# Turning v into token order: four TensorE transposes and a ScalarE copy, against a VectorE block transpose and a trip through DRAM

## The chip, the cores and the metric

The kernel runs on one NeuronCore of one Trainium2 chip. The time is the device time of one execution of the program in microseconds (us). Five instruction streams run side by side and meet through semaphores: TensorE (PE in the rows, its weight loads PEld), VectorE (DVE), ScalarE (ACT), GpSimd (POOL) and SyncE (SP, whose instructions here are almost all DMA issues, SPq in the rows).

## The reference, cut to what matters

```python
q = silu(x @ Wq); k = silu(x @ Wk); v = silu(x @ Wv); z = x @ Wz      # x: 2048 tokens x 512, W: 512 x 2048
q, k, v = causal_conv4(q), causal_conv4(k), causal_conv4(v)           # depthwise, 4 taps
q, k = rope(q), rope(k);  q, k = q / |q|, k / |k|                     # 16 heads of 128
out = 0
for s in range(4):                                                    # the token itself and 3 before it
    attn = einsum("bshd,bshd->bsh", q, lag(k, s)) * scale
    out = out + (attn * sigmoid(lag(a, s) * b))[..., None] * lag(v, s)
out = out * rms(out) * norm_w * silu(z)
s = out @ Wout
x = x + s * silu(ffn(xn))                                             # xn: layernorm of x; the x above is xn too
```

## The kernel before, in words

The work on q, k, v, z and the attention is done in 64 steps: for each of 16 heads `h` four groups `g` of 512 tokens, `c = 4h + g`. Heads 0, 1 and 15 are written out, heads 2 to 14 are one hardware loop with four steps in its body. In such a step the channels of a head lie on the 128 partitions and the 512 tokens along the free dimension. After the 64 steps follow the feed-forward part and the output projection, which the change leaves alone.

Every engine has a hand-written order of its own for a step (`step` in `on_sync`, `on_gpsimd`, `on_scalar`, `on_vector`, `on_tensor`), and the steps overlap: while q, k and v of step c are made, the rest of the steps c-1, c-2 and c-3 is done.

- TensorE, step c: twelve matmuls each for q, k and v (`project`, L982; operands split in a high and a low part), `turn_fold` (L1050, four transposes of summed squares, c-1), twelve for z (c-2), `turn_v` (L1026, four transposes of v, c-1), `sum_values` (L1038, c-3, in two halves of a matrix bank), `score` (L1060, c-2). Then q of step c+1.
- ScalarE: SiLU of the q bank into `u_q` (L636), the first tap into `y_q` (L651); the same for k and v; squares of q and k, SiLU of z, `copy_v` (L668: the transposed v from its bank into `v_tok`), a small spill.
- VectorE: the taps 1 to 3 of q, 1 to 3 of k, 1 and 2 of v (L800), and between them the three parts of rope (L820, L824, L827), `sum_fold` (L833), `gate_scores` and `mask_band` (L841 and L850, which make `coef`, the weights of `sum_values`), `join_out` and `make_o` (L806, L858), and at g = 1 and 3 the low parts of the next weights (L811: z at g = 1, q, k and v at g = 3).
- GpSimd: adds the fourth tap to `y_v` and sums squares, both by an accumulating DMA; makes norms and `gates` (L534).
- SyncE: the half swaps of q and k for rope (L425), the reciprocal norms through a DRAM scratch and back (`store_rq` L392 to L395, `load_rq` L402, whose result `gates` is made from), `o_buf` to DRAM (`store_o`, L406), next weights (L411).

`sum_values` of step c multiplies `v_tok` of c-3 with `coef` of c-3, and `coef` is made by VectorE in the same step c:

```python
wait(pe, coef_done, c - 2)
wait(pe, v_tok_done, c - 2)
wait(pe, o_done, c - 3)
wait(pe, out_sq_done, c - 3)
```

Inside the hardware loop `c` is a register, so the value that such a wait compares with has to be computed by an instruction of the engine's own sequencer (REGISTER_ALU or ISA in the rows of instructions); values already at hand in a register are used again.

Of the kernel before, what the change touches and what calls it, by code (L numbers as in the profile page):

```python
# [6 lines left out]
def gated_recurrent_block_kernel(  # L7
# [64 lines left out]
    o_scratch = nc.dram_tensor("o_scratch", [HD, S], fp32).ap()  # L72
    rq_scratch = nc.dram_tensor("rq_scratch", [G, P + LAGS, BC], fp32).ap()
# [131 lines left out]
def attention(nc, env):  # L205
# [10 lines left out]
     ones, ones_set, o_stored, o_done, out_sq_done, sq_added, rq_scratch, ffn) = (  # L216
# [4 lines left out]
                         "sq_added", "rq_scratch", "ffn"))  # L221
# [5 lines left out]
    HALF = D // 2  # L227
    bank_qv, bank_kz = banks[0], banks[1]
    bank_tqv, bank_tk = banks[2], banks[3]
# [74 lines left out]
    turned_v = sem("turned_v")  # L304
    norms_done = sem("norms_done")
    v_tok_done = sem("v_tok_done")
# [23 lines left out]
    last_tap_added = sem("last_tap_added")  # L330

# [29 lines left out]
    def on_sync(sp):  # L361
# [41 lines left out]

        def store_o(h3, g3, k):
# [8 lines left out]
        def step(h, g):  # L413
# [38 lines left out]
    def on_gpsimd(pool):  # L452
# [89 lines left out]
        def add_last_tap(g1, c):  # L542
            wait(pool, last_tap_made, c)
            wait(pool, conv_done["v"], 2 * c)
            wait(pool, turned_v, c - 1)
# [35 lines left out]
    def on_scalar(act):  # L581
# [51 lines left out]
        def silu_and_tap(n, bank, h, g, c):  # L633
# [6 lines left out]
            if n == "v":  # L640
                wait(act, last_tap_added, 16 * (c - 1))
                wait(act, turned_v, c - 1)
# [21 lines left out]

        def copy_v(g1, c):
            wait(act, turned_v, c)
            wait(act, out_done, c - 3)
            nc.scalar.activation(v_tok[:, g1 * BC:(g1 + 1) * BC, :],  # L668
                                 bank_tqv[:, :].rearrange("p (b d) -> p b d", b=BC),
                                 ACT.Copy).then_inc(v_tok_done, 1)  # L670
# [29 lines left out]
        def step(h, g):  # L700
# [15 lines left out]
            if at := back(h, g, 1):  # L716
                copy_v(at[1], c)
# [21 lines left out]
        copy_v(G - 1, NC)  # L739
# [19 lines left out]
    def on_vector(dve):  # L759
# [76 lines left out]

        def gate_scores(g2, k):
# [25 lines left out]
        def step(h, g):  # L863
# [39 lines left out]
            conv_tap("v", 1, h, g, c)  # L903
            if is_start(h, g):
# [27 lines left out]
        schedule(dve, step)  # L932
        rope("k", 1, G - 1, NC - 1)
# [20 lines left out]
    def on_tensor(pe):  # L954
# [64 lines left out]
        def turn_v(g1, c):  # L1019
            wait(pe, v_tok_done, c - 1)  # L1020
            if isinstance(c, int) and c == NC:
                pe.wait_ge(conv_done["v"], 2 * NC + 1)
# [581 lines left out]
```

## Time and profile before

| | |
|---|---|
| median of 3 runs | 1341.99 us (1341.51 to 1342.49) |
| profiled execution | 1341.58 us |
| span of its instructions | 1339.8 us |
| PE busy | 1316.8 us, 98% |
| DVE busy | 956.3 us, 71% |
| ACT busy | 782.0 us, 58% |
| POOL busy | 472.3 us, 35% |
| DMA engines, all queues | 31.9% SyncE's, 22.2% GpSimd's |

The span runs from the first instruction to the last, and the 1.8 us between it and the profiled time lie around it. Busy shares are means over stages that differ: the 64 steps end at about 925 us, and in them VectorE is busy 90% of the time, after them far less. PE's clock is granted in full throughout.

### The profile page before, as it was taken

To read this page: it belongs to the slowest core of one execution; us is meant where nothing else is said; L and a number is where in the kernel's file an instruction comes from. 1 tells how busy PE (TensorE), PEld (TensorE's weight loads), DVE (VectorE), ACT (ScalarE), POOL (GpSimd) and SP (SyncE) were. 2 spreads that over 40 slices of the span, in tenths; PEclk is the share of its full clock that TensorE was granted. 3 is DMA by queue.
4 is the path that set the end of the run, shared out by engine and by line. 5 is a ranking of instruction groups with operands and counts; after the bars stand their busy time and mean duration, and the time that the engine had idled before them with its cause. 6 is when DMAs were issued, how large, how long until landed. Compare 5 with 4: busy or idle time off the path is not lost.

```text
span 1339.8 us, 22528 instructions
## 1 busy us (share of the span) xinstructions
PE 1316.8 (98%) x6568; PEld 1102.9 (82%) x6568; DVE 956.3 (71%) x1531; ACT 782.0 (58%) x1504; POOL 472.3 (35%) x634
## 2 busy tenths in 40 slices
PE   7999999999999999999999999999999999999998
PEld 5688888888888888888888888887888888888886
DVE  7898999989998999889998999986122222324442
ACT  5676766667666766667676776665544434422221
POOL 6254545544544544545554455543000000000001
PEclk9999999999999999999999999999999999999999
DMA  8366667566666566565666657556610101256543
GB/s 264 85 126 132 135 123 154 129 128 138 134 138 146 120 136 148 121 147 121 146 139 130 139 118 158 105 121 172 207 40 24 47 16 55 70 166 206 179 131 137
DMA packets 141562, 171.83 MB, mean 128 GB/s; under 512 B 32720, under 2 KB 69584, under 8 KB 141264
## 3 DMA queue, kind: packets, MB, share of 16 engines
q1 hardware_dynamic: 114160, 121.48, 31.9%
q0 software_dynamic: 27360, 49.82, 22.2%
q8 instruction: 23, 0.38, 0.1%
q14 instruction: 19, 0.16, 0.0%
HBM read 62.58 MB, written 25.30 MB: 66 GB/s over the span
## 4 chain that ended last, share of the span: by engine, by line
PE 95%; DVE 1%; issue 1%; DMA 1%; POOL 1%; ACT 1%; SPq 0%; POOLq 0%; DVEq 0%; ACTq 0%
PE bank L982 50%; PE bank L1489 13%; PE bank L1292 9%; PE bank L1279 8%; PE bank L1038 4%; PE bank L1060 4%; PE bank L1050 2%; PE bank L1026 2%; PE bank L972 1%; DMA down_raw<-in_x 1%; PE bank L959 0%; PE bank L998 0%; POOL rnorm L510 0%; DMA down_raw<-down_raw 0%; PE bank L120 0%
## 5 line engine op out<-in xcount | busy, mean ns | idle before, releaser
L800 DVE SCALAR_TENSOR_TENSOR y_q<-u_q,cw_q,y_q 128x512 f32<-128x512 f32 x192 | 143.1, 745 | 70.9 <-ACT y_q L651 70.7
L1268 DVE TENSOR_TENSOR hid_lo<-relu,hid_hi 128x512 fp32r<-128x512 f32 x64 | 44.3, 693 | 168.2 <-ACT hid_hi L1260 168.1
L800 DVE SCALAR_TENSOR_TENSOR y_k<-u_k,cw_k,y_k 128x512 f32<-128x512 f32 x192 | 143.2, 746 | 1.5 <-ACT y_k L651 1.4
L1360 POOL TENSOR_TENSOR g_buf<-g_buf,up_raw 128x512 f32<-128x512 f32 x3 | 3.8, 1281 | 356.2 <-DVE g_buf L1420 356.2
L1256 ACT ACTIVATE relu<-bank,us_sb 128x512 f32<-128x512 f32 x64 | 44.1, 690 | 123.3 <-PE bank L1279 123.3
L510 POOL TENSOR_TENSOR rnorm<-norms,neg_half 128x8 f32<-128x8 f32 x64 | 109.0, 1703 | 9.6 <-POOL norms L506 8.6
L1380 ACT ACTIVATE hid_hi<-o_raw 128x512 fp32r<-128x512 f32 x64 | 40.2, 630 | 115.9 <-PE bank L1489 100.8
L553 POOL DMA_DIRECT2D down_raw<-down_raw x63 | 58.9, 935 | 131.8 <-ACT down_raw L691 128.4
L636 ACT ACTIVATE u_q<-bank 128x512 f32<-128x512 f32 x64 | 38.4, 600 | 110.4 <-PE bank L982 110.3
L1440 DVE TENSOR_TENSOR hid_lo<-o_raw,hid_hi 128x512 fp32r<-128x512 f32 x64 | 43.8, 690 | 79.9 <-ACT hid_hi L1380 79.9
L1489 PE MATMUL bank<-x_hi,hid_hi 128*128 128x512 f32 x256 | 99.6, 389 | 0.0
L1489 PE MATMUL bank<-x_hi,hid_lo 128*128 128x512 f32 x256 | 99.6, 389 | 0.0
L1489 PE MATMUL bank<-x_lo,hid_hi 128*128 128x512 f32 x256 | 99.6, 389 | 0.0
L800 DVE SCALAR_TENSOR_TENSOR y_v<-u_v,cw_v,y_v 128x512 f32<-128x512 f32 x129 | 96.0, 744 | 0.0
L506 POOL TENSOR_SCALAR norms<-norms 128x8 f32<-128x8 f32 x64 | 33.5, 523 | 137.9 <-DVE norms L833 137.9
L636 ACT ACTIVATE u_v<-bank 128x512 f32<-128x512 f32 x64 | 38.4, 600 | 72.1 <-PE bank L982 72.1
L1292 PE MATMUL bank<-down_sign_b,hid_hi 128*128 128x512 f32 x192 | 74.8, 390 | 0.4 <-DVE hid_lo L1268 0.4
L1292 PE MATMUL bank<-down_sign_b,hid_lo 128*128 128x512 f32 x192 | 74.7, 389 | 0.0
L982 PE MATMUL bank<-x_hi,whi_z 128*128 128x512 f32 x256 | 74.6, 413 | 0.0
L982 PE MATMUL bank<-x_hi,whi_q 128*128 128x512 f32 x252 | 73.5, 413 | 0.1
L547 POOL DMA_DIRECT2D y_v<-down_raw x63 | 73.3, 1164 | 0.4 <-issue 0.4
L1038 PE MATMUL bank<-coef,v_tok 128*128 128x132 f32 x512 | 69.7, 279 | 1.8 <-ACT swapped_q L683 0.4
(193 smaller groups left out, 3650.1 us busy)
## 6 DMA issues: line engine op xcount, KB each, us to landing
swapped_q<-y_q SPq DMA_DIRECT2D x128, 128.0 KB, 2.8
swapped_k<-y_k SPq DMA_DIRECT2D x128, 128.0 KB, 2.3
o_scratch<-o_buf SPq DMA_DIRECT2D x64, 256.0 KB, 4.2
o_raw<-o_scratch SPq DMA_DIRECT2D x64, 256.0 KB, 4.2
down_raw<-down_raw POOLq DMA_DIRECT2D x63, 256.0 KB, 3.4
y_v<-down_raw POOLq DMA_DIRECT2D x63, 256.0 KB, 5.0
sq_sum<-out_sq POOLq DMA_DIRECT2D x62, 256.0 KB, 3.8
raw_q<-in_wq SPq DMA_DIRECT2D x16, 256.0 KB, 4.1
```

The costliest lines, as they stand in the source:

```text
L510: nc.gpsimd.tensor_tensor(rnorm[:, g1 % 2, :], norms[:, g1 % 2, :], neg_half[:, 0:2 * BC], ALU.pow).then_inc(root_done, 1)
L547: nc.gpsimd.dma_start(y["v"][:, g1 % 2, :], last_tap[:, g1 % 2, :], accum_op=ALU.add).then_inc(last_tap_added, 16)
L553: nc.gpsimd.dma_start(fold, other, accum_op=ALU.add).then_inc(folded, 16)
L636: nc.scalar.activation(u[n][:, g % 2, HALO:], bank[:, :], ACT.Silu).then_inc(silu_done[n], 1)
L800: nc.vector.scalar_tensor_tensor(y[n][:, g % 2, :], u[n][:, g % 2, i:i + CH], cw[n][:, bass.ds(h * TAPS + i, 1)], y[n][:, g % 2, :], ALU.m ...
L982: last = nc.tensor.matmul(bank[:, :], w[n][:, i % KT, :], part[:, i % KT, cols(g)], start=(i == 0), stop=(i == TERMS - 1))
L1038: last = nc.tensor.matmul(two[:, b // 2, at:at + BW], v_tok[:, g3 * BC + b, :], coef[:, g3 % 2, b, :], start=(b % 2 == 0), stop=(b % 2 == ...
L1060: last = nc.tensor.matmul(scores[:, b, :], rot["k"][:, at:at + P], rot["q"][:, at:at + BW], start=True, stop=True)
L1268: nc.vector.tensor_tensor(hid_lo[:, j % HS, :], relu[:, j % 2, :], hid_hi[:, j % HS, :].bitcast(fp32), ALU.subtract).then_inc(hid_lo_done, 1)
L1279: last = nc.tensor.matmul(up_bank(n, j), up_group(j // WG)[:, t, j % WG * P:(j % WG + 1) * P], part[:, t, bass.ds(n * CH, CH)], start=(k = ...
L1292: last = nc.tensor.matmul(acc_of(n)[b], part[:, j % HS, b * P:(b + 1) * P], down_group(j // WG)[:, j % WG, :], start=(j == 0 and part is h ...
L1489: last = nc.tensor.matmul(sums[b], part[:, h % HS, b * P:(b + 1) * P], wo_tile(w, h // KT, h % KT), start=(h == 0 and k == 0), stop=(h == ...
```

## The change

`turn_v` moves from TensorE to VectorE, and `copy_v` of ScalarE goes. VectorE's transpose works on squares of 32 by 32 inside `y_v`, in place (`nc.vector.transpose`, 128x512). The squares themselves are then at the wrong places, which a transfer mends: SyncE stores the 256 KB to `v_scratch` in DRAM and loads them back into `v_tok` with four DMAs, one for each 32 partitions, in runs of 32 numbers (128 bytes). The first wait of `sum_values` on `v_tok` is now one on that load.

```diff
+    v_scratch = nc.dram_tensor("v_scratch", [2, P, CH], fp32).ap()
...
+    SQUARE, RUNS = 32, P // 32
...
+    def wait_v(eng, g, c):
+
+        wait(eng, v_in[g % 2], 16 * RUNS * (c // 2 + 1) if isinstance(c, int) else
+             c * 8 * RUNS + (16 if g % 2 == 0 else 8) * RUNS)
...
+        def store_v(g1, k):
+            wait(sp, v_turned, k + 1)
+            sp.dma_start(v_scratch[g1 % 2], y["v"][:, g1 % 2, :]).then_inc(v_stored, 16)
+
+        def load_v(g1, k):
...
+            wait(sp, v_stored, 16 * (k + 1))
+            squares = v_scratch[g1 % 2].rearrange("(i a) (b j d) -> j a b i d", a=SQUARE, b=BC, d=SQUARE)
+            to_tok = v_tok[:, g1 * BC:(g1 + 1) * BC, :].rearrange("p b (i d) -> p b i d", d=SQUARE)
+            for j in range(RUNS):
+                sp.dma_start(to_tok[j * SQUARE:(j + 1) * SQUARE, :, :, :], squares[j]).then_inc(v_in[g1 % 2], 16)
...
             if at := back(h, g, 1):
+                store_v(at[1], c - 1)
                 store_rq(at[1], c)
             if at := back(h, g, 2):
                 load_rq(at[1], c)
             if at := back(h, g, 3):
                 store_o(at[0], at[1], c - 3)
+            if at := back(h, g, 1):
+                load_v(at[1], c - 1)
...
+        store_v(G - 1, NC - 1)
         sp.wait_ge(turned_f, NC)
         env["load_down"](sp, 0)
         store_rq(G - 1, NC)
+        load_v(G - 1, NC - 1)
         load_rq(G - 2, NC, rq_late_in[0])
...
-            if at := back(h, g, 1):
-                copy_v(at[1], c)
...
+        def turn_v(g1, k):
+
+            if isinstance(k, int) and k == NC - 1:
+                wait(dve, conv_done["v"], 2 * NC + 1)
+            else:
+                wait(dve, last_tap_added, 16 * (k + 1))
+            if not (isinstance(k, int) and k < 2):
+                wait_v(dve, g1, k - 2)
+            v = y["v"][:, g1 % 2, :]
+            nc.vector.transpose(v, v).then_inc(v_turned, 1)
...
             conv_tap("v", 1, h, g, c)
+            if at1:
+                turn_v(at1[1], c - 1)
...
             wait(pe, coef_done, c - 2)
-            wait(pe, v_tok_done, c - 2)
+            wait_v(pe, g3, c - 3)
...
-            if at1:
-                turn_v(at1[1], c)
             if at3:
                 sum_values(at3[1], c)
```

The instruction streams show where this lands. First TensorE, in the loop's body, from the end of z to `sum_values`. Of the kernel before, position g = 0 of the body, with the waits that each instruction carries:

```order
L982 MATMUL bank<-x_lo,whi_z 128x512 x4
L1026 MATMUL bank<-const,y_v 128x128 [waits last_tap_added,v_tok_done]
L1026 MATMUL bank<-const,y_v 128x128 x3
L79 REGISTER_ALU [waits v_tok_done,coef_done]
L1038 MATMUL bank<-coef,v_tok 128x132 [waits out_sq_done,o_done]
L1038 MATMUL bank<-coef,v_tok 128x132 x3
```

Here a register instruction holds the wait for `coef`, and the matmul follows it. The same place of the kernel before at position g = 1; g = 2 and 3 read the same:

```order
L982 MATMUL bank<-x_lo,whi_z 128x512 x4
L1026 MATMUL bank<-const,y_v 128x128 [waits last_tap_added,v_tok_done]
L1026 MATMUL bank<-const,y_v 128x128 x3
L1038 MATMUL bank<-coef,v_tok 128x132 [waits o_done,out_sq_done,v_tok_done,coef_done]
L1038 MATMUL bank<-coef,v_tok 128x132 x3
```

Here the matmul itself holds all four waits, since every value stands in a register already. The changed kernel at g = 1; all four positions of its loop read so at this place:

```order
L1013 MATMUL bank<-x_lo,whi_z 128x512 x4
L80 ISA [waits coef_done]
L1058 MATMUL bank<-coef,v_tok 128x132 [waits out_sq_done,o_done,v_in0]
L1058 MATMUL bank<-coef,v_tok 128x132 x3
L1080 MATMUL bank<-rot_q,rot_k 128x132 [waits gated,rope_done_k,rope_done_q]
```

The transposes are gone, and the wait for `coef` stands on a register instruction ahead of the matmul at all four positions, where it was one of four before. In the heads that are written out it stays on the matmul.

Second VectorE, loop position g = 3, from the low part of the next q weights. Before:

```order
L811 TENSOR_TENSOR wlo_q<-raw_q,whi_q 128x512 [waits whi_done_q]
L800 SCALAR_TENSOR_TENSOR y_v<-u_v,cw_v,y_v 128x512 [waits tap_done_v]
L79 REGISTER_ALU
L820 TENSOR_TENSOR rot_q<-y_q,cos 128x512 [waits scores_done,conv_done_q]
L79 ISA
```

The same place of the changed kernel:

```order
L828 TENSOR_TENSOR wlo_q<-raw_q,whi_q 128x512 [waits whi_done_q]
L817 SCALAR_TENSOR_TENSOR y_v<-u_v,cw_v,y_v 128x512 [waits tap_done_v]
L80 REGISTER_ALU
L80 ISA [waits last_tap_added]
L863 STREAM_TRANSPOSE y_v<-y_v 128x512 [waits v_in0]
L80 REGISTER_ALU
L837 TENSOR_TENSOR rot_q<-y_q,cos 128x512 [waits scores_done,conv_done_q]
```

The transpose has come in behind the first v tap; `mask_band` of the same step is ahead of this piece, `make_o` and the next step's q taps are behind it.

Third SyncE, one step of head 1 in the changed kernel, from the k swap on. Before, the same piece has neither the `v_scratch` row nor the `v_tok` rows:

```order
L447 DMA swapped_k<-y_k 64x512 [waits rope_done_k,conv_done_k]
L447 DMA swapped_k<-y_k 64x512
L414 DMA v_scratch<-y_v 128x512 [waits v_turned]
L400 DMA rq_scratch<-rnorm 128x4 [waits root_done]
L401 DMA rq_scratch<-rnorm 4x3
L403 DMA rq_scratch<-rnorm 4x1
L410 DMA rq_win<-rq_scratch 128x1x32 [waits rq_stored]
L428 DMA o_scratch<-o_buf 128x512 [waits o_done]
L424 DMA v_tok<-v_scratch 32x16x32 [waits v_stored]
L424 DMA v_tok<-v_scratch 32x16x32 x3
```

The store stands ahead of the reciprocal norms, with its wait; the four loads stand last, ahead of the next step's swaps and, at g = 0 and 2, of the next weights.

## Rows read from the trace of the kernel before

**Rows 1.** The page's chain that ended last, by line.
```profile
span 1339.8 us, 22528 instructions
...
PE bank L982 50%; PE bank L1489 13%; PE bank L1292 9%; PE bank L1279 8%; PE bank L1038 4%; PE bank L1060 4%; PE bank L1050 2%; PE bank L1026 2%; PE bank L972 1%; DMA down_raw<-in_x 1%; PE bank L959 0%; PE bank L998 0%; POOL rnorm L510 0%; DMA down_raw<-down_raw 0%; PE bank L120 0%
```

**Rows 2.** Steps g=0, g=1: busy PE, PEld, DVE, ACT, POOL; clock, DMA share, GB/s.
```profile
305.48:319.48 14.00, 13.86 (x76) 11.62 (x74) 13.74 (x24) 9.82 (x20) 6.83 (x9) 1.00 0.77 172
319.48:333.12 13.64, 13.64 (x75) 11.59 (x74) 11.71 (x20) 8.80 (x19) 6.80 (x9) 1.00 0.55 114
```

**Rows 3.** Timeline of VectorE over one head: q tap, gate_scores, mask_band; start, duration.
```profile
111.08 0.71 DVE L850 TENSOR_TENSOR coef<-coef,const 128x528 f32<-128x528 f32 x1
...
296.37 0.75 DVE L800 SCALAR_TENSOR_TENSOR y_q<-u_q,cw_q,y_q 128x512 f32<-128x512 f32 x1 [1.64 <-ACT y_q L651]
...
310.18 0.75 DVE L800 SCALAR_TENSOR_TENSOR y_q<-u_q,cw_q,y_q 128x512 f32<-128x512 f32 x1
...
316.00 0.69 DVE L841 TENSOR_TENSOR coef<-bank,gates 128x528 f32<-128x528 f32 x1
316.73 0.71 DVE L850 TENSOR_TENSOR coef<-coef,const 128x528 f32<-128x528 f32 x1
...
323.98 0.75 DVE L800 SCALAR_TENSOR_TENSOR y_q<-u_q,cw_q,y_q 128x512 f32<-128x512 f32 x1 [1.65 <-ACT y_q L651]
...
330.53 0.71 DVE L850 TENSOR_TENSOR coef<-coef,const 128x528 f32<-128x528 f32 x1
...
337.60 0.75 DVE L800 SCALAR_TENSOR_TENSOR y_q<-u_q,cw_q,y_q 128x512 f32<-128x512 f32 x1 [0.99 <-ACT y_q L651]
```

**Rows 4.** Timeline of TensorE and its weight loads around sum_values (L1038).
```profile
111.84 0.97 PEld L1038 LDWEIGHTS bank<-coef,v_tok 128*128 128x128 f32 x8 [0.19 <-DVE coef L850]
...
317.65 0.97 PEld L1038 LDWEIGHTS bank<-coef,v_tok 128*128 128x128 f32 x8 [0.35 <-issue]
...
330.96 0.60 PE L1026 MATMUL bank<-const,y_v 128*128 128x128 f32 x4
...
331.29 0.98 PEld L1038 LDWEIGHTS bank<-coef,v_tok 128*128 128x128 f32 x8
...
333.12 1.17 PE L982 MATMUL bank<-x_hi,whi_q 128*128 128x512 f32 x4
```

**Rows 5.** Groups of VectorE instructions by line: busy us, mean ns.
```profile
L820 DVE TENSOR_TENSOR rot_k<-y_k,cos 128x512 f32<-128x512 f32 x64 | 43.6, 681 | 0.0
...
L773 DVE TENSOR_SCALAR rot_k<-rot_k,coef 128x512 f32<-128x512 f32 x4 | 4.2, 1049 | 0.3 <-POOL coef L464 0.3
```

**Rows 6.** Timeline of SyncE and GpSimd: the reciprocal norms' way, and a weight load.
```profile
305.39 0.59 SPq L392 DMA_DIRECT2D rq_scratch<-rnorm  x1
...
308.18 0.57 SPq L402 DMA_DIRECT2D rq_win<-rq_scratch  x1
...
310.63 1.29 SPq L411 DMA_DIRECT2D raw_k<-in_wk  x1
...
311.83 0.51 POOL L534 TENSOR_TENSOR gates<-rq_own,gate_k 128x16 f32<-128x16 f32 x1 [0.16 <-POOL rq_own L529]
```

**Rows 7.** DMA: SyncE's queue in 313.4 to 315.5 us, then over the span; an issue's landing.
```profile
q1 hardware_dynamic: 1014, 0.50, 83.7%
...
q1 hardware_dynamic: 114160, 121.48, 31.9%
...
o_scratch<-o_buf SPq DMA_DIRECT2D x64, 256.0 KB, 4.2
```

**Rows 8.** Timelines behind the last step: VectorE's gate_scores, SyncE's late load, TensorE's score.
```profile
918.84 0.71 DVE L841 TENSOR_TENSOR coef<-bank,gates 128x528 f32<-128x528 f32 x1 [3.43 <-POOL gates L534]
...
923.66 0.71 DVE L841 TENSOR_TENSOR coef<-bank,gates 128x528 f32<-128x528 f32 x1 [0.71 <-POOL gates L534]
...
919.53 1.22 SPq L402 DMA_DIRECT2D rq_win<-rq_scratch  x2
...
925.22 1.06 PE L1060 MATMUL bank<-rot_q,rot_k 128*128 128x132 f32 x8
```

More of the change, by code:

```diff
@@ L215, in attention @@
      cw, gate0, raw, w_hi, w_lo, raw_in, whi_done, wlo_done, w_slice, nw_sb, us_sb, o_scratch, up_raw, down_raw,
-     ones, ones_set, o_stored, o_done, out_sq_done, sq_added, rq_scratch, ffn) = (
+     ones, ones_set, o_stored, o_done, out_sq_done, sq_added, rq_scratch, v_scratch, ffn) = (
         env[n] for n in ("const", "neg_half", "x_hi", "x_lo", "sq_sum", "ident", "sel_own", "sel_next", "band",
@@ L220, in attention @@
                          "up_raw", "down_raw", "ones", "ones_set", "o_stored", "o_done", "out_sq_done",
-                         "sq_added", "rq_scratch", "ffn"))
+                         "sq_added", "rq_scratch", "v_scratch", "ffn"))
     (cos, sin, y, rot, v_tok, coef, u, swapped, norms, rnorm, rq_win, rq_own, gate_k, gates, z_act, out_sq, o_buf,
@@ L227, in attention @@
     HALF = D // 2
+    SQUARE, RUNS = 32, P // 32
     bank_qv, bank_kz = banks[0], banks[1]
-    bank_tqv, bank_tk = banks[2], banks[3]
+    bank_tk = banks[3]
     HALF_CH = CH // 2
@@ L303, in attention @@
     turned_f = sem("turned_f")
-    turned_v = sem("turned_v")
+    v_turned = sem("v_turned")
     norms_done = sem("norms_done")
-    v_tok_done = sem("v_tok_done")
+    v_stored = sem("v_stored")
+    v_in = [sem(f"v_in{i}") for i in range(2)]
     floor_done = sem("floor_done")
@@ L402, in load_rq @@
             sp.dma_start(rq_win[:, g2 % 2, :, :].rearrange("p j b -> p (j b)"), runs).then_inc(arrived, 16)
+        def store_v(g1, k):
+            wait(sp, v_turned, k + 1)
+            sp.dma_start(v_scratch[g1 % 2], y["v"][:, g1 % 2, :]).then_inc(v_stored, 16)
+        def load_v(g1, k):
+            if isinstance(k, int) and k == 0:
+                sp.wait_ge(picked, 2)
+            wait(sp, v_stored, 16 * (k + 1))
[3 more added lines that the diff above has]
+                sp.dma_start(to_tok[j * SQUARE:(j + 1) * SQUARE, :, :, :], squares[j]).then_inc(v_in[g1 % 2], 16)
         def store_o(h3, g3, k):
@@ L544, in add_last_tap @@
             wait(pool, conv_done["v"], 2 * c)
-            wait(pool, turned_v, c - 1)
+            wait(pool, v_turned, c - 1)
             pool.sem_inc(last_tap_asked, 1)
@@ L641, in silu_and_tap @@
                 wait(act, last_tap_added, 16 * (c - 1))
-                wait(act, turned_v, c - 1)
+                wait(act, v_stored, 16 * (c - 1))
             else:
@@ L663, in on_scalar @@
         nc.scalar.activation(w_hi["z"][:, :, :], raw["z"][:, :, :], ACT.Copy).then_inc(whi_done["z"], 1)
[L665 to L670, printed above, removed]
         def save_spill(g3, c):
@@ L738, in on_scalar @@
         silu_z(G - 2, NC - 2, bank_kz)
-        copy_v(G - 1, NC)
         for n in "qk":
@@ L932, in on_vector @@
         schedule(dve, step)
+        turn_v(G - 1, NC - 1)
         rope("k", 1, G - 1, NC - 1)
@@ L1017, in on_tensor @@
         pe.wait_ge(cleared, 6)
[L1019 to L1022, printed above, removed]
-            else:
-                wait(pe, last_tap_added, 16 * c)
-            for b in range(BC):
-                last = nc.tensor.transpose(bank_tqv[:, b * P:(b + 1) * P],
-                                           y["v"][:, g1 % 2, b * P:(b + 1) * P], ident)
-            last.then_inc(turned_v, 1)
         def sum_values(g3, c):
             wait(pe, coef_done, c - 2)
-            wait(pe, v_tok_done, c - 2)
+            wait_v(pe, g3, c - 3)
             wait(pe, o_done, c - 3)
@@ L1105, in on_tensor @@
         turn_fold(NC)
-        turn_v(G - 1, NC)
         wait(pe, silu_done["v"], 2 * NC)
@@ L1120, in on_tensor @@
         pe.wait_ge(z_done, NC)
-        pe.wait_ge(v_tok_done, NC)
         pe.wait_ge(gated, NC)
```

## The prediction, made before the changed kernel was run

> **What bounds the kernel now.** I read the chain that ended last first. Its row gives the four transposes of v (L1026) 2% of 1339.8 us, some 26.8 us or 0.42 us in each of 64 steps, and nearly all else is TensorE too [rows 1]. Read alone, it promises 27 us. The windows agree at first sight: PE is busy 13.64 of 13.64 us at g = 1 [rows 2]. But a full engine is not yet the only bound, so I followed the timelines through one step to see what the last instruction before each meeting point waits for.
>
> There is a loop of dependences through three engines that is as long as TensorE's work. From VectorE's first q tap (323.98) to `mask_band` (starts 330.53) are 6.55 us, and it takes 0.71, so it ends at 331.24 [rows 3]. The weight load of `sum_values`, which needs that result, starts at 331.29, 0.05 later. From there `sum_values` and `score` take until q of the next step starts at 333.12 (1.83 us) [rows 4]. From that to the next q tap of VectorE, which waited 0.99 us for ScalarE's first tap of this very q, are 4.48 us (337.60) [rows 3]. The sum, 6.55 + 0.71 + 0.05 + 1.83 + 4.48 = 13.62 us, is the period. None of these five pieces holds a transpose of v: `turn_v` starts at 330.96 and lies beside `mask_band` [rows 4]. It fills time in which TensorE would otherwise wait.
>
> The step from g = 3 to g = 0 is bound differently. VectorE has three low parts of weights more, and its row at 310.18 shows no wait: from 296.37 it works 13.81 us through. Its `mask_band` (316.73 + 0.71 = 317.44) is then late [rows 3], and the load of `sum_values` starts at 317.65, with 0.35 idle put down to issue [rows 4]. That is 0.21 after the end, not 0.05. A case in head 1, which is written out, had a stall as well (0.19 idle for L850) and started at 111.84, 0.05 after the end at 111.08 + 0.71 [rows 3, 4]. The streams in the section on the change tell why, as I read it: at g = 0 of the loop a register instruction stands between the wait and the matmul, so a TensorE that really waits pays 0.16 us more; where the matmul holds the waits it doesn't.
>
> **The change part by part.**
> Taken off TensorE: 0.42 us a step. By the loop above it is worth nothing at any step. Instead TensorE arrives at `coef`'s wait early and waits about 0.4 us.
>
> The wait on `coef` now stands on a register instruction at all four loop positions, and TensorE now waits at all of them. At g = 0 the 0.16 us is already in the time. For g = 1 and g = 2 it is new, 2 x 0.16 = 0.32 us for each of the 13 loop heads; at g = 3 it delays TensorE, but the next q tap waits for VectorE itself, not for TensorE. From below this could be 0, if the 0.21 has another cause.
>
> Added to VectorE: one transpose, T. The trace has none of its kind. An ordinary pass over 128x512 takes 0.681 us; the slowest group of that size is a tensor_scalar at 1.049 [rows 5]. It can't be free, since it reads and writes as much as these, nor a gain. Neighbours on the engine overlap a little, so the nearest row makes 0.65 of it, and that I take. Below I keep 0.5, for a pass with one operand less; above, twice the pass, 1.3, in case a square has to be filled before it is written. Behind g = 0, 1 and 2 VectorE waits 1.65, 0.99 and 1.64 us for the next q tap [rows 3], which hides T. Behind g = 3 there is no wait, so the whole of T lengthens 13.81 us. That is 0.65 for each loop head, and once each for heads 0 to 1 and 14 to 15, where the low parts are written out. With T above 0.99 + 0.16 the step g = 1 would pay the excess too.
>
> One rule speaks against T. The Trainium skill, "VectorE: DVE Perf Modes", section "The three transpose paths", gives 311 ns for a 128x128 bf16 transpose on VectorE; four of them make an estimate of 1.24 us, against the 0.65 that I take from the row. No row before shows which is right; with it the sum would be 11 us higher, the rival below.
>
> Taken off ScalarE: `copy_v`. VectorE's q tap waits for ScalarE's tap, but ScalarE itself waits for the q bank before that, and ACT is busy only 8.80 of 13.64 us [rows 2]. Worth 0.
>
> Added to SyncE: `store_v` and four loads. `store_v` waits for a transpose that ends about when `store_rq` used to begin, and its 256 KB go ahead of the reciprocal norms in the same queue; such a store lands in 4.2 us [rows 7]. Before, the norms' stores start at 305.39, their load at 308.18, and `gates` is done at 312.34, 3.66 us before `gate_scores` wants it at 316.00 [rows 3, 6]. I reckon 0.65 for the wait and issue, and up to 1.6 for the landing (4.2 less the 2.8 between 305.39 and 308.18, and 0.2 for the small stores behind it): 2.2 of 3.66 us. Hidden, with 1.4 to spare. The loads stand last. Each issue costs between 0.57 (128 short runs) and 1.29 us (512 runs) [rows 6]; four take some 3 us on a SyncE that then goes on to the swaps, which rope reads one step later. `sum_values` wants `v_tok` two steps later. Worth 0.
>
> Packets: 2048 of 128 bytes and 128 of 2 KB a step. In a stretch full of 512-byte packets, 1014 of them took 83.7% of 16 engines for 2.1 us, 28 ns each; over the span the queue's mean is 0.319 x 1339.8 x 16 / 114160 = 60 ns [rows 7]. A short packet is nearest to the first: 2048 x 28 ns / 16 = 3.6 us, and at most 0.5 for the store, on the 0.55 (0.77 at g = 0) of some 13.7 us that the engines are busy now [rows 2], about 8.5 us: 12.6 of 13.9, and just over full at g = 0. Close, but a transfer that nobody waits for may take its time. The Trainium skill, "DMA: Bandwidth & Descriptors", Specifications, says that below 512 bytes an engine reads, modifies and writes. No row here separates that.
>
> Behind the last step VectorE is on the path: its `sum_fold` is now two transposes late (2 x 0.65), and `gate_scores` at 918.84, which waits on `gates` that come from it, moves by 1.3. The four loads of the last v stand ahead of the late loads of the norms at 919.53, some 3 us of issue and 1 us of packets. The `gate_scores` at 923.66 then comes at about 927.9 and the `score` behind it at 928.7 instead of 925.22 [rows 8]: 3.5 us in all. From below 1.3.
>
> Sum: 13 x (0.65 + 0.32) = 12.6, 2 x 0.65 = 1.3, and 3.5: 17.4 us. On the profiled 1341.58 that is 1359.0; the median of the runs is 0.4 above that execution. I predict **1359**.
>
> **The rivals.**
> *The bound stays, the prices differ* is the forecast's own spread: T = 0.5, no price for the register instruction and 1.3 behind the last step give 15 x 0.5 + 1.3 = 8.8, so 1350; T = 0.8 with the rest as taken gives 1361. Chance 0.52 for 1350 to 1365.
>
> *A slow transpose.* At twice the pass, T = 1.3, g = 3 pays 0.65 more 15 times (9.8), g = 1 pays 1.3 - 0.99 - 0.16 = 0.15 (13 times, 2.0), the end 1.3: 1372. With the slowest row's 1.05 it would be 1366. For it speaks that a square must be full before its first column can leave, against it only the likeness to other passes. Chance 0.12 for 1365 to 1373. The skill's 311 ns, named above, would land in this case, at 1370.
>
> *The norms come late.* If `store_v` holds the reciprocal norms back by more than 3.66 us, `gate_scores` and with it `mask_band`, which lies on the loop, slip by the excess in each step. Half a microsecond makes 32 us more, 1390; one makes 1420. For it: the store, the fold and the fourth tap all run in the same 4 us, with the DMA engines at 0.77 at g = 0 already. Against it: 1.4 us to spare by my sum. Chance 0.20.
>
> *The DMA engines become the bound.* At 60 ns a packet, 7.7 us a step on top of 0.55 to 0.77 of 13.7 (about 8.5 us) plus 0.5: 16.7 us against 13.9, some 180 us over 64 steps, 1540. It decides from (13.9 - 9.0) x 16 / 2048, about 38 ns a packet. Chance 0.05.
>
> *Faster: TensorE was the only bound.* If `mask_band` could end earlier, or its end is recorded later than it releases, TensorE's 0.42 us come off each step, less T at g = 3: 64 x 0.42 = 27, less 15 x (0.65 - 0.42) = 3.5, and 3.5 behind: about 1322. The same 0.05 us between end and load at a place with a stall and one without speaks against it. It decides if TensorE's load could start clearly ahead of 331.24. Chance 0.05.
>
> *No change.* The low end's loss of 8.8 us, and some of that handover after all: 0.1 us less in each of 64 steps gives 6.4 back, 1344. Chance 0.06.
>
> **How the numbers follow.** This kernel's measurement tells about 0.2%, 2.7 us, from no change. Faster holds the 0.05, same the 0.06, slower the other 0.89. The range reaches from the low end of the forecast, 1349, over the slow transpose to norms half a microsecond late, 1390; it leaves out faster, no change, DMA-bound and half of the late norms, about 0.2. The forecast's own range is 1350 to 1365.
>
> **What the new profile would show.** Right: a wait of TensorE's weight load of `sum_values` at every step, 0.2 to 0.4 us, released by `mask_band` or put down to issue; PE less busy, while the period is 13.8 us at three positions of a head and about 14.45 in one; VectorE without a q tap wait at g = 0 and near 95% busy; transposes of 0.6 to 0.75. Wrong: periods near 13.2 (TensorE was the bound); `gate_scores` waiting for `gates` (late norms), or swaps landing in 6 us or more and waited for by VectorE (DMA).

## The result, and the profile after

The changed kernel takes 1357.55 us (median of 4 runs, 1356.91 to 1358.84) against 1341.86 in the same session: 1.0118 times, 95% interval 1.01 to 1.0135. It is slower. The profiled execution took 1357.75 us, with a span of 1355.8, 16.0 more than before.

The head of its page, with busy times and TensorE's granted clock:

```profile
span 1355.8 us, 22340 instructions
...
PE 1305.5 (96%) x6312; PEld 1072.8 (79%) x6312; DVE 989.5 (73%) x1595; ACT 752.3 (55%) x1440; POOL 486.7 (36%) x634
...
PEclk9989999999999999999999999999999999999999
```

TensorE is busy for 11 us less in 16 us more time. One digit of its clock is an 8, to which I come below. The windows of the steps g = 0 and g = 1 of one head (columns as in [rows 2]):

```profile
312.37:326.63 14.26, 13.65 (x71) 11.04 (x70) 14.10 (x24) 9.09 (x19) 7.57 (x9) 1.00 0.81 180
326.63:340.35 13.72, 13.44 (x72) 11.13 (x70) 12.34 (x21) 8.33 (x18) 7.01 (x9) 1.00 0.83 178
```

They were 14.00 and 13.64 long. VectorE is full in the first, and the DMA engines went from 0.77 and 0.55 to 0.8. The timeline of VectorE in these steps, which answers to [rows 3]:

```profile
309.61 0.71 DVE L878 TENSOR_TENSOR coef<-coef,const 128x528 f32<-128x528 f32 x1
...
312.16 0.70 DVE L863 STREAM_TRANSPOSE y_v<-y_v 128x512 f32<-128x512 f32 x1
312.79 0.65 DVE L837 TENSOR_TENSOR rot_q<-y_q,cos 128x512 f32<-128x512 f32 x1
...
317.38 0.75 DVE L817 SCALAR_TENSOR_TENSOR y_q<-u_q,cw_q,y_q 128x512 f32<-128x512 f32 x1
...
323.86 0.71 DVE L878 TENSOR_TENSOR coef<-coef,const 128x528 f32<-128x528 f32 x1
...
331.13 0.75 DVE L817 SCALAR_TENSOR_TENSOR y_q<-u_q,cw_q,y_q 128x512 f32<-128x512 f32 x1 [1.11 <-ACT y_q L678]
...
337.58 0.71 DVE L878 TENSOR_TENSOR coef<-coef,const 128x528 f32<-128x528 f32 x1
```

The transpose takes 0.70 us and the next instruction starts 0.63 behind it. Its group over the whole span (busy us, mean ns of one):

```profile
L863 DVE STREAM_TRANSPOSE y_v<-y_v 128x512 f32<-128x512 f32 x64 | 45.0, 703 | 0.0
```

The q tap at 317.38 has no wait (g = 0); the next one waits 1.11. The weight loads of `sum_values` that wait for `mask_band`, and q of the step behind, from TensorE's timeline:

```profile
324.80 0.97 PEld L1058 LDWEIGHTS bank<-coef,v_tok 128*128 128x128 f32 x8 [0.90 <-issue]
...
326.63 1.17 PE L1013 MATMUL bank<-x_hi,whi_q 128*128 128x512 f32 x4
...
338.52 0.97 PEld L1058 LDWEIGHTS bank<-coef,v_tok 128*128 128x128 f32 x8 [0.68 <-issue]
```

`mask_band` ends at 324.57 and 338.29, the loads start 0.23 us later both times; before, it was 0.21 at g = 0 and 0.05 elsewhere [rows 3, 4]. The view of waits (us in total, times, longest) sums it up:

```profile
DVE y_q L817 <- ACT y_q L678: 50.1, 47, 4.3
...
PEld bank L1058 <- issue: 39.8, 53, 0.9
PE bank L1058 <- DVE coef L878: 19.9, 59, 0.5
DVE coef L869 <- POOL gates L561: 6.7, 2, 3.4
```

The weight-load side of TensorE stands idle for 0.75 us on average ahead of `sum_values`, 53 times; its matmuls wait there for 0.34 us on average. VectorE waited for `gates` twice only, both behind the last step: the norms aren't late in the steps. In GpSimd's timeline of the step g = 0 they come at 321.37, and `gate_scores` starts at 323.13:

```profile
320.89 0.48 POOL L561 TENSOR_TENSOR gates<-rq_own,gate_k 128x16 f32<-128x16 f32 x1 [0.16 <-POOL rq_own L556]
```

The starts of q in the timeline tell where the 16.0 us lie. The step of head 0 that begins near 58 us takes 19.44 instead of 15.24: 4.2. Ahead of it and in the rest of heads 0 and 1: 0.9, so that the loop starts at 145.98 instead of 140.92. Of this, 0.65 lies ahead of that step (57.96 instead of 57.31), where executions differ by more than that without the change too: 58.47 in experiment 11. The 13 loop heads: 55.47 instead of 54.88 us each on average, 0.59 x 13 = 7.7. Head 15 and what lies behind the last step: 0.2 and 3.1.

The step in head 0 follows, from the timelines of TensorE and GpSimd. Before (L1050 is `turn_fold`, then z, then `turn_v`; the POOL rows are the product `gate_k` and the issue of the fold, the transfer that `turn_fold` waits for):

```profile
64.05 0.21 POOL L515 TENSOR_TENSOR gate_k<-gate,rnorm 128x16 f32<-128x16 f32 x1 [3.53 <-DVE gate L927]
64.56 0.93 POOL L553 DMA_DIRECT2D down_raw<-down_raw  x1 [0.30 <-issue]
...
68.05 0.63 PE L1050 MATMUL bank<-const,down_raw 128*128 128x128 f32 x4 [1.50 <-DMA down_raw<-down_raw]
68.43 1.18 PE L982 MATMUL bank<-x_hi,whi_z 128*128 128x512 f32 x4
...
71.29 0.60 PE L1026 MATMUL bank<-const,y_v 128*128 128x128 f32 x4
```

After:

```profile
65.29 1.26 POOL L542 TENSOR_TENSOR gate_k<-gate,rnorm 128x16 f32<-128x16 f32 x1 [4.12 <-DVE gate L957]
...
66.50 0.91 POOL L580 DMA_DIRECT2D down_raw<-down_raw  x1
...
65.66 1.07 PE L1013 MATMUL bank<-x_lo,whi_v 128*128 128x512 f32 x4
70.66 1.09 PE L1070 MATMUL bank<-const,down_raw 128*128 128x128 f32 x4 [3.94 <-DMA down_raw<-down_raw]
71.40 2.06 PE L1013 MATMUL bank<-x_hi,whi_z 128*128 128x512 f32 x4
...
76.58 1.07 PE L1080 MATMUL bank<-rot_q,rot_k 128*128 128x132 f32 x8
```

and the window behind it:

```profile
70.00:80.00 10.00, 9.34 (x35) 7.81 (x36) 5.83 (x9) 3.11 (x5) 3.77 (x5) 0.68 0.52 132
```

GpSimd stands in a wait for VectorE's `gate`, then makes the product `gate_k`, and the fold is queued behind both. Counted from the step's first matmul of q (57.31 before, 57.96 after), the fold is issued at 8.54 us instead of 7.25, 1.3 later. T accounts for 0.6 of it: the product starts at 7.33 instead of 6.74. The product itself takes 1.26 us instead of 0.21, and of these 1.05 us the gap of 0.3 ahead of the issue hides a part. TensorE idles for 3.94 us, where it idled for 1.50, and then its granted clock is 0.68 over 10 us, a mean between its two levels of 1.2 and 2.4 GHz; in the kernel before it is 1.00 in the same window. z took 2.86 us (68.43 to 71.29) and takes 5.18 (71.40 to 76.58). So of the 4.2 us, 2.3 are z at the lower clock, and the rest is the later fold, less the `turn_v` that is gone.

### The profile page after: what moved, and what is told of

Read it like the earlier page. It is cut to its first block, busy times and chain, and to the rows that moved or that the text cites. A ratio compares the mean times of both kernels' runs of the same rounds, so it can differ in the third digit from the quotient of the medians.

```text
span 1355.8 us, 22340 instructions
## 1 busy us (share of the span) xinstructions
PE 1305.5 (96%) x6312; PEld 1072.8 (79%) x6312; DVE 989.5 (73%) x1595; ACT 752.3 (55%) x1440; POOL 486.7 (36%) x634
## 4 chain that ended last, share of the span: by engine, by line
PE 49%; DVE 31%; issue 11%; ACT 5%; DMA 1%; SPq 1%; DVEq 1%; POOL 1%; POOLq 0%; ACTq 0%
PE bank L1505 13%; PE bank L1013 11%; PE bank L1308 8%; PE bank L1295 8%; DVE y_k L817 7%; DVE y_q L817 5%; PE bank L1058 4%; DVE rot_k L844 3%; PE bank L1080 3%; DVE coef L869 3%; DVE coef L878 2%; ACT y_q L678 2%; DVE rot_q L844 2%; ACT u_q L663 2%; DVE y_v L817 2%
## 5 line engine op out<-in xcount | busy, mean ns | idle before, releaser
L553 POOL TENSOR_TENSOR rq_win<-rq_win,const 128x32 f32<-128x32 f32 x64 | 43.5, 680 | 218.7 <-DMA rq_win<-rq_scratch 218.7
L537 POOL TENSOR_TENSOR rnorm<-norms,neg_half 128x8 f32<-128x8 f32 x64 | 113.3, 1771 | 9.6 <-POOL norms L533 8.6
L1058 PEld LDWEIGHTS bank<-coef,v_tok 128*128 128x128 f32 x512 | 62.3, 189 | 45.1 <-issue 39.8
L1058 PE MATMUL bank<-coef,v_tok 128*128 128x132 f32 x512 | 73.0, 286 | 20.5 <-DVE coef L878 19.9
```

The source lines that it names most:

```text
L537: nc.gpsimd.tensor_tensor(rnorm[:, g1 % 2, :], norms[:, g1 % 2, :], neg_half[:, 0:2 * BC], ALU.pow).then_inc(root_done, 1)
L1058: last = nc.tensor.matmul(two[:, b // 2, at:at + BW], v_tok[:, g3 * BC + b, :], coef[:, g3 % 2, b, :], start=(b % 2 == 0), stop=(b % 2 == ...
```

## The experiments

In the first session the kernel before had a median of 1341.81 us, in the second 1342.33, in the third 1342.48. Lengths of steps ("periods") are distances of q's first matmul in TensorE's timeline, given in the order g = 0 to 3; "per head" is their sum, as a mean over the 13 loop heads.

**1. no_turn.** The kernel before without `turn_v` on TensorE; `copy_v` reads `y_v` itself.

```diff
-            if at1:
-                turn_v(at1[1], c)
...
-            wait(act, turned_v, c)
+                wait(act, last_tap_added, 16 * c)
...
-                                 bank_tqv[:, :].rearrange("p (b d) -> p b d", b=BC),
+                                 y["v"][:, g1 % 2, :].rearrange("p (b d) -> p b d", b=BC),
```

> The kernel before, with the four transposes of v left out: ScalarE copies y_v as it lies into v_tok (so v isn't in token order), and nothing is put on VectorE or the DMA queues. This is the gain of the change alone, without its costs. If the loop TensorE q, ScalarE tap, VectorE q tap to mask_band, sum_values, score is what bounds a step: no change, 1342, at most 3 us less, with a wait of about 0.4 us ahead of sum_values at every step. If TensorE's own work was the bound: 64 x 0.42 = 27 us less, 1315.

Measured: 1340.01 us, ratio 0.9986 (0.9977 to 0.9995). Periods of a head 13.94, 13.53, 13.60, 13.62. In the timeline of a step g = 3, VectorE's `mask_band` and TensorE's load behind it:

```profile
303.10 0.71 DVE L853 TENSOR_TENSOR coef<-coef,const 128x528 f32<-128x528 f32 x1
...
303.86 0.97 PEld L1041 LDWEIGHTS bank<-coef,v_tok 128*128 128x128 f32 x8 [0.57 <-DVE coef L853]
```

TensorE is done with z half a microsecond early and waits until 0.05 behind `mask_band`. The 27 us that the chain put on the transposes are not there. This settles it: the loop of dependences is the bound, and the removal is worth 1.8 us.

**2. wait_last.** The changed kernel with the wait for `coef` named last.

```diff
-            wait(pe, coef_done, c - 2)
             wait_v(pe, g3, c - 3)
             wait(pe, o_done, c - 3)
             wait(pe, out_sq_done, c - 3)
+            wait(pe, coef_done, c - 2)
```

> The changed kernel, with the four waits of sum_values in another order, coef_done last, so that all of them stand on the matmul at all four loop positions and no register instruction follows the wait for coef. If the register instruction costs 0.16 us wherever TensorE really waits: 0.16 less at g = 0, 1 and 2 of 13 loop heads, 6.2 us, so 1351, and the weight load 0.05 behind mask_band in place of 0.22. If the 0.22 is how a stalled TensorE starts: no change, 1357.5.

Measured: 1354.54 us, 1.009 (1.0076 to 1.0103), 3 less than the change, where 6.2 were expected. Per head 55.12 instead of 55.47. The load now starts 0.12 behind `mask_band` (307.88 + 0.71, then 308.71), neither 0.22 nor 0.05: so the instruction that holds the wait is a cost, but my expectation had it wrong which one that is here. In this kernel's stream a semaphore instruction just ahead of the matmul holds the wait for `coef`, and the matmul itself only the one for the load of v. Where the matmul itself holds the wait for `coef` (the kernel before at g = 1 to 3, and no_dram there, where the load really waits), the load starts 0.05 behind `mask_band`; where a register instruction holds it, with a semaphore instruction between it and the matmul (the changed kernel, and the kernel before at g = 0), 0.21 to 0.23. The rows in the section on the change name, beside a matmul, the waits of such semaphore instructions too; of the four waits at g = 1 there, only that for `coef` is the matmul's own.

The last q starts 4.95 us earlier, and 2.5 of that are lost again behind the last step: the second `gates` there start 32.6 us behind the last q instead of 31.7, TensorE idles for 2.59 us ahead of the `score` that needs them instead of 1.72, and then its granted clock falls, which it doesn't in the changed kernel:

```profile
937.00:942.00 5.00, 4.80 (x22) 4.57 (x23) 3.73 (x7) 1.30 (x4) 1.53 (x2) 0.66 0.75 213
```

The eight matmuls of `score` take 1.75 us there instead of 1.14, and the eight of `sum_values` 1.97 instead of 1.06. Why the second `gates` come later no run separates.

**3. no_dve_turn.** The changed kernel with a tiny copy (0.16 us) in the place of the transpose.

```diff
-            nc.vector.transpose(v, v).then_inc(v_turned, 1)
+            nc.vector.tensor_copy(v[0:32, 0:2], v[0:32, 0:2]).then_inc(v_turned, 1)
```

> The changed kernel, with a copy of 32x2 numbers in place of VectorE's transpose (so the squares aren't turned); the store and the loads stay. If VectorE pays for the transpose only behind g = 3, in head 0 and behind the last step: 15 x 0.6 = 9, 4 at the start of head 0 and 1 at the end, 14 us less, 1343.5. If the DMA traffic were what costs: hardly any less, 1355 or more.

Measured: 1354.93 us, 1.01 (1.0084 to 1.0115). The expectation misses by 11 us, and it is the most useful miss. Two q taps of VectorE around g = 3 to g = 0:

```profile
303.10 0.75 DVE L817 SCALAR_TENSOR_TENSOR y_q<-u_q,cw_q,y_q 128x512 f32<-128x512 f32 x1 [1.71 <-ACT y_q L678]
...
317.08 0.75 DVE L817 SCALAR_TENSOR_TENSOR y_q<-u_q,cw_q,y_q 128x512 f32<-128x512 f32 x1 [0.17 <-ACT y_q L678]
```

13.98 us apart, and the second waits for 0.17. Without T, VectorE is done in some 13.8 us there, and the loop of dependences, with the register instruction in it at g = 3 too, is longer than that. Taking T out of this kernel therefore gives back 0.31 us a head (55.16 against 55.47), not 0.65. And the step in head 0 got longer still, 20.98 instead of 19.44: the product `gate_k` started 6.80 us behind the step's q, as early as in the kernel before (6.74), but took 4.45 us instead of 1.26. So the stall there doesn't need T. Behind the last step 0.9 us more were lost; why stays open.

**4. no_dram.** The changed kernel without the store and the loads: ScalarE copies `y_v` into `v_tok` at the end of its step.

```diff
-                store_v(at[1], c - 1)
...
-                load_v(at[1], c - 1)
...
+                copy_v(at[1], c)
...
-            wait_v(pe, g3, c - 3)
+            wait(pe, v_stored, c - 2)
```

> The changed kernel, without the trip through DRAM: VectorE transposes the squares, and ScalarE copies y_v as it lies into v_tok at the end of its step (so the squares aren't put in order). If the DMAs cost nothing but the late norms behind the last step (some 2 us) and the register instruction that their wait brings (at g = 1 and 2, 4 us): 1351.5. If they also slow the steps by contention: 1345 or less, with a shorter VectorE chain from q tap to mask_band.

Measured: 1351.88 us, 1.0076 (1.0062 to 1.009), as expected. A head takes 55.21 us, against 55.12 in wait_last, where 256 KB still go out and come back in each step. The two kernels hand `coef` over differently: here the load starts 0.21 us behind `mask_band` at g = 0 and 0.05 elsewhere, in wait_last 0.11 to 0.12 everywhere. From VectorE's q tap to the next one, less that hand-over, the steps g = 0 to 2 take 13.48, 13.51 and 13.53 us here and 13.49, 13.50 and 13.54 in wait_last (medians over the loop). The trip through DRAM costs the loop nothing there. At g = 3 VectorE takes 14.36 us here and 14.26 in wait_last; this 0.1 is not explained.

**5. late_load_v.** The changed kernel with the loads of the last v issued behind the late loads of the norms.

```diff
-        load_v(G - 1, NC - 1)
         load_rq(G - 2, NC, rq_late_in[0])
         sp.wait_ge(rq_joined, NC - 2)
         load_rq(G - 1, NC, rq_late_in[1])
+        load_v(G - 1, NC - 1)
```

> The changed kernel with the four loads of the last v issued behind the late loads of the reciprocal norms, behind the last step. Theory: their issue (2.7 us) and their packets no longer stand ahead of the load that the last gate_scores waits for, some 2 us less: 1355.5. Rival (the end is late for the two transposes and for VectorE's order alone): no change, 1357.5; if the last sum_values then waits for v, slower.

Measured: 1356.52 us, 1.0103 (1.0088 to 1.0119). That is 1 us less than the change, within the spread of its runs; in the profiled executions the stretch behind the last q is 0.4 us shorter (447.15 instead of 447.51). SyncE's timeline shows why it gives so little. The changed kernel:

```profile
931.05 0.63 SPq L414 DMA_DIRECT2D v_scratch<-y_v  x1
...
933.11 0.30 SPq L403 DMA_DIRECT2D rq_scratch<-rnorm  x1
933.86 3.01 SPq L424 DMA_DIRECT2D v_tok<-v_scratch  x4
936.91 1.29 SPq L410 DMA_DIRECT2D rq_win<-rq_scratch  x2
```

late_load_v:

```profile
932.97 0.30 SPq L403 DMA_DIRECT2D rq_scratch<-rnorm  x1
936.70 1.23 SPq L410 DMA_DIRECT2D rq_win<-rq_scratch  x2
```

The load of the norms starts 3.50 and 3.43 us behind the end of their stores' issue, with or without the four issues between. It waits for the stores to land, and these lie behind 256 KB of `v_scratch` and the previous `v_tok` loads; before, it was 0.86 us, from 918.67 to 919.53 [rows 8]. Experiment 12, which moves the 256 KB behind them, bears this out.

**6. gate_later.** The changed kernel with the product `gate_k` of head 0's first group moved behind the next step's fold and fourth tap.

```diff
                 add_last_tap(at[1], c)
+                if is_start(h, g - 2):
+                    pool.wait_ge(gate_done, 2)
+                    gate_keys(0, 0, 1)
...
-                if is_start(h, g - 1):
-                    pool.wait_ge(gate_done, 2)
-                gate_keys(at[0], at[1], c)
+                if not is_start(h, g - 1):
+                    gate_keys(at[0], at[1], c)
```

> The changed kernel with one product of GpSimd in head 0, gate_k of the first group, which waits for VectorE's gate, moved behind the fold of the squares and the fourth tap of the next step. The step of head 0 that begins near 58 us takes 19.44 us in the changed kernel and 15.24 in the one before. Theory (GpSimd is held by that wait and by the product itself, which took between 0.21 and 4.45 us in the runs so far, and the fold issued behind it comes late, so that TensorE idles and its granted clock falls to 0.68): the fold is issued as early as before or earlier, the step takes 15.3 or less, the clock stays full, 4.2 us less: 1353.4. Rival (the fold is late for the queues, since the load of v and the store stand in them too): the step stays above 17 us and the time above 1355.

Measured: 1351.8 us, 1.007 (1.0056 to 1.0084), 5.8 less than the change. The fold in GpSimd's timeline, and the window at 70:

```profile
63.42 0.93 POOL L580 DMA_DIRECT2D down_raw<-down_raw  x1 [2.19 <-ACT down_raw L713]
```

```profile
70.00:80.00 10.00, 10.00 (x52) 8.47 (x51) 9.68 (x16) 5.58 (x12) 5.52 (x7) 1.00 0.74 157
```

The step takes 13.24 us, less than the 15.24 of before, and the clock stays full. That settles the cause in head 0: the wait for `gate` and the product stood ahead of the fold.

**7. scores_early.** wait_last, with `gate_scores` and `mask_band` ahead of the third k tap on VectorE.

```diff
-            conv_tap("k", 2, h, g, c)
             if at3:
                 gate_scores(at3[1], c - 3)
                 mask_band(at3[1], c - 3)
+            conv_tap("k", 2, h, g, c)
```

> The changed kernel with two edits: the wait for coef is named last, so that it stands on the matmul, and VectorE makes gate_scores and mask_band ahead of the third k tap instead of behind it. The piece of the loop of dependences from the q tap to the end of mask_band loses one tap, about 0.66 us. Theory (the loop is the bound and TensorE merely waits in it): periods fall to TensorE's own work without the transposes, 13.64 - 0.42 = 13.22 us, with some 0.6 us more in one step of a head for VectorE's low parts; 53.5 us a head against 55.51 in the changed kernel, 13 heads 26 us, so about 1330, below both kernels. Rival (gates come too late): gates are done at about q + 9.0 to 9.4 us and gate_scores would want them at q + 9.6; if GpSimd is the next to be late, VectorE waits for gates and the time stays between 1345 and 1355. Rival (VectorE is full): above 93% busy it is the bound itself, and nothing is won, 1354.

Measured: 1335.2 us, 0.9947 (0.9933 to 0.996): faster than both kernels, though 5 above the forecast; the step in head 0 still takes 18.26 us. The window of a step g = 1, and `mask_band` and the load of a step g = 3:

```profile
319.63:332.80 13.17, 13.17 (x70) 11.06 (x69) 12.53 (x21) 8.28 (x18) 5.69 (x8) 1.00 0.85 190
```

```profile
302.52 0.73 DVE L878 TENSOR_TENSOR coef<-coef,const 128x528 f32<-128x528 f32 x1
...
303.42 1.09 PEld L1058 LDWEIGHTS bank<-coef,v_tok 128*128 128x128 f32 x8
```

`mask_band` ends 0.17 ahead of the load, which waits for nothing; at g = 1 it is so in ten of the 13 heads. TensorE is the bound at three positions (13.16 to 13.21), VectorE at the fourth (14.28).

**8. before_scores_early.** The kernel before with the same move on VectorE.

> The kernel before with the same order of VectorE alone: gate_scores and mask_band ahead of the third k tap. Theory: TensorE's work of 13.64 us is then the only bound, the 0.3 us of the step from g = 3 to g = 0 go, 54.6 us a head against 54.91, some 4.6 us over 13 heads: about 1337. That would show that the transposes of v are worth their time on TensorE only once the loop is shorter. Rival (the loop does not run through mask_band): no change, 1342.

Measured: 1338.73 us, 0.9973 (0.9963 to 0.9983). Periods 13.72 and three times 13.63: the excess of g = 0 has shrunk from 0.35 to 0.09 us; 1.7 more than forecast in time.

**9. early_wait_first.** scores_early with the wait for `coef` back in first place.

> scores_early without its other edit: the wait for coef again stands first, on a register instruction. Theory: mask_band ends at q + 10.97 us at three positions of a head, and 0.22 us behind it is 11.19, when TensorE is just done with z (its load of sum_values starts at 11.21 in scores_early), so the register instruction costs nothing there and 0.1 us at g = 0, with the heads that are written out as they are: 1336.5. Rival (the price of 0.16 us is paid wherever the instruction stands): 0.16 x 52 = 8.3 more, 1343.5.

Measured: 1336.74 us, 0.9951 (0.9938 to 0.9965). Periods 14.34 at g = 0 (0.06 more) and 13.16 to 13.19 elsewhere, as in scores_early. A register instruction costs only where TensorE really waits behind it.

**10. no_turn_early.** no_turn with the edits of 6 and 7 (of 7 the part on VectorE).

> The kernel of no_turn (no transposes of v anywhere, ScalarE copies y_v as it lies, so the values are not those of v in token order) with the order of VectorE of scores_early and GpSimd's product moved. In no_turn itself the transposes were worth 1.8 us. Theory (they are worth their time once the loop is shorter): periods of 13.2 us, at g = 0 about 13.5 since VectorE has no transpose; 0.4 to 0.45 us in each of 64 steps against before_all_edits, so 27 less: 1310. Rival (another loop of dependences of 13.5 us or more stands behind the first): 1325 or more.

Measured: 1319.22 us, 0.9824 (0.981 to 0.9837), 9 above the forecast. Periods 13.89, 13.21, 13.15, 13.15: per head 53.37, 1.2 us less than with transposes (54.60 in experiment 11), not 1.7. At g = 0 VectorE's q tap waits for nothing, so VectorE holds that step at 13.89.

**11. before_all_edits.** The kernel before with the edits of 6 and 8.

> The kernel before, transposes on TensorE, with the same order of VectorE and the same move of GpSimd's product. before_scores_early took 1338.7; its step of head 0 takes 15.23 us of which TensorE's own work is 13.64, so 1.6 less: 1337.1. Beside all_edits it says what turning v on VectorE is worth where the loop of dependences is not the bound: some 9 us.

Measured: 1337.62 us, 0.9962 (0.9948 to 0.9976), as expected. The step in head 0 takes 13.94 us instead of 15.23.

**12. all_edits.** The changed kernel with the edits of 2, 5, 6 and 7, and the last store of v behind the stores of the norms.

```diff
-        store_v(G - 1, NC - 1)
         sp.wait_ge(turned_f, NC)
         env["load_down"](sp, 0)
         store_rq(G - 1, NC)
-        load_v(G - 1, NC - 1)
+        store_v(G - 1, NC - 1)
```

> The changed kernel with the order of VectorE of scores_early, the wait of wait_last, the product of GpSimd moved as in gate_later, and behind the last step the store of the last v behind the stores of the reciprocal norms and its loads behind their late loads. Theory (the three places are apart and add up): scores_early took 1335.2; its step of head 0 of 18.26 us becomes 13.25, 5.0 less; behind the last step the late load of the norms leaves some 3 us earlier, 1 to 3 less: 1328. Rival (the stall moves on, for instance to the z weights or to gates in head 0): 1331 or more.

Measured: 1327.77 us, 0.9887 (0.9872 to 0.9902), the fastest of those that leave nothing out. The late load in SyncE's timeline:

```profile
904.51 0.29 SPq L403 DMA_DIRECT2D rq_scratch<-rnorm  x1
...
905.67 1.23 SPq L410 DMA_DIRECT2D rq_win<-rq_scratch  x2
```

It follows the stores by 0.87 us again, as before the change. Against experiment 11, turning v on VectorE is now worth 9.9 us. Against 10 it costs 8.6: 5.0 lie in the 13 loop heads (0.39 each, all of it at g = 0), and 2.4 in two steps of head 1, which take 14.39 and 14.47 us instead of 13.21 and 13.29. There `gate_scores` waits for `gates`, so in these two steps the norms do come late:

```profile
109.70 0.71 DVE L871 TENSOR_TENSOR coef<-bank,gates 128x528 f32<-128x528 f32 x1 [0.74 <-POOL gates L561]
...
124.17 0.71 DVE L871 TENSOR_TENSOR coef<-bank,gates 128x528 f32<-128x528 f32 x1 [1.32 <-POOL gates L561]
```

## Why the prediction was right, and where its sizes were off

**The loop of dependences holds no transpose of v, so their removal is worth nothing.** Right, shown by experiment 1 (1.8 us of 27), and from the other side by 7, 8 and 10: with a shorter loop the same removal brings 9.9 us (12 against 11) or 18.4 (10 against 11).

**The wait on a register instruction costs 0.16 us where TensorE really waits.** Right in place and size by the trace (0.23 against 0.05 at g = 1), and shown by 2 and 9; what lies between it and the matmul is part of it, as 2 shows. I counted it at g = 1 and 2, 0.32 a head. From one q tap of VectorE to the next, the steps g = 0 to 3 took 13.78, 13.62, 13.67 and 13.81 us before and take 13.72, 13.71, 13.77 and 14.26 (medians over the loop). So g = 1 and 2 pay 0.09 and 0.10 each: the hand-over's 0.16, less 0.06 by which VectorE is now faster from its q tap to `mask_band` (6.48 instead of 6.54), a gain that I had not foreseen and that no_turn has too at g = 0 and 1. At g = 3 nothing is paid, as I had said: the tap at 317.38 waits for nothing, and wait_last has the same 14.26.

**T = 0.65, paid in full at g = 3.** T was well sized: 0.703 us alone, 0.63 to the next start. But VectorE's step at g = 3 grew by 0.45, from 13.81 to 14.26 us. I had read the 13.81 as work without a gap, and it was not: ahead of `make_o` VectorE was idle, and that row of the kernel before, against the changed one, is

```profile
308.26 0.75 DVE L858 SCALAR_TENSOR_TENSOR o_buf<-bank,nw_sb,z_act 128x512 f32<-128x512 f32 x1 [0.22 <-DVE bank L806]
...
315.51 0.75 DVE L886 SCALAR_TENSOR_TENSOR o_buf<-bank,nw_sb,z_act 128x512 f32<-128x512 f32 x1
```

It started 0.39 us behind the instruction before it and now starts 0.29 behind; two shorter distances elsewhere in the step give the rest. The Trainium skill, "VectorE: DVE Perf Modes", section "The three transpose paths", has 311 ns for a 128x128 bf16 square; my estimate of 1.24 us from it for four is not what 128x512 of f32 took here, 0.70. Both terms together: 0.59 us a head measured, 0.97 forecast, 4.9 us too much over the loop.

**Heads 0 to 1: T once.** This is the step that failed most: 5.06 us instead of 0.65, of which 4.2 in one step. I had looked at the norms' way in the loop's steps, not at what else waits for VectorE in head 0, where a product on GpSimd stands behind VectorE's `gate` and the fold that TensorE wants stands behind the product. Experiment 6 shows that this order is the cause. T itself is only 0.6 us of the delay there; the product's own time and z at the lower clock, 2.3 of the 4.2 us, are larger, and I had thought of neither.

**The end, 3.5 us.** Measured 3.1, but only the two transposes, 1.2 of it, for the reason given: the first `gate_scores` behind the last step comes 24.68 us after the last q instead of 23.47. The second comes at 32.09 instead of 28.29, but the issue of the four loads isn't what delays its norms: late_load_v moves that and gains 0.4 us behind the last q. The norms' stores land late, behind v's packets (experiments 5 and 12).

**ScalarE's copy 0, SyncE and DMA 0 in the steps.** Right: experiments 2 and 4 have the same steps at g = 0 to 2, but for the hand-over of `coef`, with the trip and without. Norms are not late in the changed kernel: 1.76 us are to spare at g = 0, where I had reckoned 1.4 of the 3.66. In all_edits, where the steps are shorter, two of head 1 do wait for late norms. The short packets were dear by my sum (28 ns); the DMA share rose from 0.64 to 0.80 over 100 to 900 us, which is 2.3 us a step, or 2.3 x 16 / 2176 = 17 ns each.

**The signs.** TensorE waits at `sum_values` in every step of the loop, the q tap at g = 0 waits for nothing, VectorE is busy for 93% of the time from 100 to 900 us, and the transpose takes 0.70 us, as foreseen; the steps are 13.7 and 14.27 us long, where I had said 13.8 and 14.45.

Errors of 4.9 us up over the loop and 4.4 down in heads 0 and 1 nearly cancel, so 1359 against 1357.55 is closer than the working deserves: that part was luck.

## What to carry to other kernels

An operation that the chain of waits shows on the path may only fill time that the engine would wait anyway: before giving it a price, follow one step's meeting points and ask what each last instruction waits for, and try a version with the operation simply gone. Once a loop of dependences is the bound, one instruction moved off it (here two passes ahead of a third) makes the removal worth its time. Look at the first and the last repetitions by themselves, where queues hold other things, and keep bulky transfers behind small ones that somebody waits for.

## What was unexpected of the hardware

A 128x16 product on GpSimd, `gate_k`, took 0.21 us in the kernel before, 1.26 after and 4.45 in no_dve_turn, at the same place in the program. Before, it began at 64.05, in a gap of 0.16 us that VectorE spent waiting; in the other two VectorE went from one 128x512 pass with two inputs to the next without a gap. The Trainium skill, "SBUF — State Buffer", section "SBUF: two separate sides", says that such a VectorE instruction and a GpSimd instruction that reads SBUF lock each other out of a shared pair of ports for a whole instruction. In no_dve_turn the rows agree with that: the product ended at 69.19, 0.08 us behind the last of VectorE's gapless passes (68.38 + 0.73). In the changed kernel it ended at 66.55 without such a gap, and in gate_later it took 0.65 us beside passes of the same kind. No run here separates the ports from other causes.

The load of `sum_values` starts 0.05 us behind `mask_band` when the matmul itself holds the wait for `coef`, 0.11 to 0.12 with a semaphore instruction in its place, and 0.21 to 0.23 with a register instruction and a semaphore instruction behind it. The rows don't show how the last figure divides between those two.

After 3.94 us without a matmul, three groups of four z matmuls took 2.06, 1.91 and 1.78 us instead of 1.18, 1.08 and 1.08, and at 76.58 TensorE was back at its usual speed. In wait_last the granted clock fell to 0.66 in the 5 us behind a gap of 2.59 us; in the changed kernel it stayed at 1.00 behind the gap of 1.72 us at the same place.
